# Attention and mixture-of-experts kernel: the first values come ahead of the first keys in the prologue

## The reference, cut to what matters

```python
x = x + cross_attention(layernorm(x), ctx)      # 8 heads of 64
x = x + moe_ffn(layernorm(x))                   # 8 experts, top 2, and a shared expert

# cross_attention(x, ctx):
q = x @ Wq; k = ctx @ Wk; v = ctx @ Wv          # Wq 256x512, Wk and Wv 192x512
attn = softmax(q k^T / 8); out = (attn @ v) @ Wout + bout
```

## Time and profile before

| | |
|---|---|
| median of 3 runs | 1103.0 us (1100.59 to 1103.97) |
| the profiled execution, its own time | 1101.89 us |
| its span, first to last instruction | 1100.1 us |
| PE busy | 1060.9 us, 96% of the span |
| DVE, ACT, POOL busy | 741.5, 692.6, 709.1 us |
| mean granted TensorE clock | 0.986 of full speed |

### The profile page before, as it was taken

The page is one execution under the profiler, slowest core; times in us unless marked ns, Lnnn a source line. Parts: engine busy times, 40 slices in busy tenths (PEclk is TensorE's granted clock), DMA queues, the critical chain, the costliest instruction groups (busy, mean ns, idle before and its releaser), DMA issues. The chain is left out here.

```text
span 1100.1 us, 25508 instructions
## 1 busy us (share of the span) xinstructions
PE 1060.9 (96%) x7342; PEld 928.8 (84%) x7342; DVE 741.5 (67%) x1937; ACT 692.6 (63%) x1649; POOL 709.1 (64%) x661
## 2 busy tenths in 40 slices
PE   5899999999999999999999889999999999999996
PEld 4688888888888888888887789999888888888886
DVE  3688888888888888888888767656533433433432
ACT  4788888888888888888887554332344343343442
POOL 2988898889888988898888556655033323332233
PEclk9999999999999999999999998989999999999999
DMA  7114313431343134313522285223483354334861
GB/s 216 47 32 140 124 55 99 139 124 53 101 139 120 55 103 139 120 52 105 177 90 76 98 293 187 97 76 126 136 225 57 55 136 90 55 55 64 266 175 15
DMA packets 83985, 124.06 MB, mean 113 GB/s; under 512 B 7904, under 2 KB 48080, under 8 KB 83920
## 3 DMA queue, kind: packets, MB, share of 16 engines
q1 hardware_dynamic: 63664, 99.86, 28.0%
q0 software_dynamic: 11760, 15.15, 7.7%
q10 hardware_dynamic: 8496, 8.22, 2.6%
HBM read 74.44 MB, written 49.68 MB: 113 GB/s over the span
## 5 line engine op out<-in xcount | busy, mean ns | idle before, releaser
L563 POOL TENSOR_TENSOR probs<-probs,first_rows 112x750 f32<-112x750 f32 x128 | 184.0, 1438 | 64.3 <-DVE first_rows L1020 63.2
L1802 POOL DMA_INDIRECT out<-stage,to_row x48 | 74.9, 1560 | 177.4 <-ACT stage L1854 125.9
L2083 DVE TENSOR_TENSOR hT_lo<-banks,hT_hi 128x512 fp32r<-128x512 f32 x63 | 43.6, 692 | 185.1 <-ACT hT_hi L1846 179.2
L755 ACT ACTIVATE probs<-banks,first_rows 112x375 f32<-112x375 f32 x256 | 145.2, 571 | 17.7 <-DVE first_rows L1007 15.5
L1007 DVE TENSOR_REDUCE first_rows<-banks 112x2 f32<-112x750 f32 x128 | 119.6, 935 | 28.1 <-PE banks L1392 26.3
L520 POOL TENSOR_TENSOR v_both<-v_raw,v_both 125x512 fp32r<-125x512 f32 x96 | 123.6, 1288 | 7.5
L1013 DVE TENSOR_TENSOR pT<-banks,pT 125x672 fp32r<-125x672 f32 x128 | 108.8, 850 | 17.9 <-ACT pT L746 16.7
L516 POOL TENSOR_TENSOR v_both<-v_raw,one 125x512 fp32r<-125x512 f32 x96 | 110.7, 1153 | 12.7 <-ACT v_raw L668 12.6
L1406 PEld LDWEIGHTS banks<-pT,v_both 125*128 125x128 f32 x768 | 99.6, 192 | 17.4 <-issue 9.3
L1406 PE MATMUL banks<-pT,v_both 125*128 125x224 f32 x768 | 110.7, 280 | 2.2 <-DVE oT_lo L1038 1.7
L1418 PE MATMUL banks<-ident,probs 112*125 112x112 f32 x768 | 106.7, 275 | 2.1 <-POOL probs L563 1.3
(11 more groups left out here) (287 smaller groups left out, 3067.8 us busy)
## 6 DMA issues: line engine op xcount, KB each, us to landing
w_split_scratch<-stage SPq DMA_DIRECT2D x16, 1536.0 KB, 6.6
ring<-w_split_scratch SPq DMA_DIRECT2D x16, 1536.0 KB
stage<-in_L_ffn_W SPq DMA_DIRECT2D x48, 256.0 KB, 2.9
ctx_in<-in_ctx SPq DMA_DIRECT2D x32, 376.0 KB, 3.8
xg<-x_sorted_scratch ACTq DMA_DIRECT2D x59, 136.0 KB
x_in<-in_x SPq DMA_DIRECT2D x16, 224.0 KB, 3.3
x_res<-in_x SPq DMA_DIRECT2D x32, 112.0 KB, 2.1
x_scratch<-x SPq DMA_DIRECT2D x32, 112.0 KB, 1.9
```

Source lines behind the costliest of these rows:

```text
L563: pool.tensor_tensor(probs[:, two, :], probs[:, two, :], inv_sum[:, 2 * s:2 * s + 2].rearrange("p (e o) -> p e o", o=1).to_broadcast([N, 2 ...
L755: act.activation(probs[:, h % 4, :], S_BANKS[0:N, e, 0:M], ACT.Exp, bias=neg_max[:, h:h + 1], accum_out=row_sum[:, h:h + 1]).then_inc(exp_ ...
```

## The change

The prologue's order is changed, and with it the order of the loads, of the splits of the weights and of who makes them. The two value units now come first, the first two key units second, then `xt`, then the other two key units, then `q0`. `AW` is renumbered, so that weights 0 and 1 are Wv and 2 and 3 are Wk. SP loads Wv, Wk, `x`, Wq, context 1, Wout, bias, and then the shared expert's weights, without waiting. ACT splits weights 0 to 5 before its first unit, normalises ahead of `k00`, and splits Wout after the prologue. DVE makes the low parts of all eight weights, 0 to 3 ahead of the statistics, 4 and 5 behind them, 6 and 7 at the prologue's end; POOL makes none.

```diff
-PROLOGUE = ["k00", "k10", "k20", "k30", "xt", "v00", "v10", "q0"]
+PROLOGUE = ["v00", "v10", "k00", "k10", "xt", "k20", "k30", "q0"]
-        AW = [("k", 0), ("k", 1), ("v", 0), ("v", 1), ("q", 0), ("q", 1), ("o", 0), ("o", 1)]
+        AW = [("v", 0), ("v", 1), ("k", 0), ("k", 1), ("q", 0), ("q", 1), ("o", 0), ("o", 1)]
@@ SP
             load_ctx(0, 0)
+            load_weight(Wv, 0, "v", True)
+            load_weight(Wk, 2, "k", True)
             sp.dma_start(x_in[:], x_rows(0, 2)).then_inc(x_loaded, 16)
-            load_weight(Wk, 0, "k", True)
-            load_weight(Wv, 2, "v", True)
             load_weight(Wq, 4, "q", False)
+            load_ctx(1, 1)
             (Wout, bias)
-            load_ctx(1, 1)
+            load_expert(sp, Ws1, Ws3, Ws2, weights_in[1])
             (router, x_res, wait xn_ready, x_in, wait ctx_lo_ready, contexts 2 and 3)
-            load_expert(sp, Ws1, Ws3, Ws2, weights_in[1])
@@ POOL
             rstd_of(1)
-            split_lo(pool, 2)
             for n, name in enumerate(PROLOGUE):
                 (split_values of the value units)
-            for n in (6, 7):
-                split_lo(pool, n)
@@ ACT
             ctx_hi(0, 1)
+            for i in range(6):
+                split_hi(i)
             for n, name in enumerate(PROLOGUE):
-                if name == "xt":
+                if name == "k00":
                     normed(1)
-                for i in {"k00": range(6), "k10": (6, 7)}.get(name, ()):
-                    split_hi(i)
                 (unit)
                 if name == "k30":
                     ctx_hi(1, 1)
+            for i in (6, 7):
+                split_hi(i)
@@ DVE
+            ctx_lo(0, 1)
+            for i in range(4):
+                split_lo(dve, i)
             statistics(1)
+            for i in (4, 5):
+                split_lo(dve, i)
             for n, name in enumerate(PROLOGUE):
-                if name == "k00":
-                    ctx_lo(0, 1)
-                    for i in (0, 1, 3):
-                        split_lo(dve, i)
-                    for i in (4, 5):
-                        split_lo(dve, i)
                 (unit of all but values; ctx_lo(1, 1) after k30)
+            for i in (6, 7):
+                split_lo(dve, i)
@@ PE
+                if name == "v00":
+                    pe.wait_ge(ctx_lo_ready[0], 1)
+                    pe.wait_ge(aw_lo["v"], 2)
                 if name == "k00":
-                    pe.wait_ge(ctx_lo_ready[0], 1)
                     pe.wait_ge(aw_lo["k"], 2)
-                if name == "v00":
-                    pe.wait_ge(aw_lo["v"], 2)
```

## The result

| | before | after |
|---|---|---|
| median (4 runs each) | 1103.43 us | 1094.33 us |
| range | 1100.59 to 1103.97 | 1092.91 to 1097.37 |
| ratio, 95% interval | | 0.9934, 0.9912 to 0.9956 |
| profiled execution, span | 1101.89, 1100.1 | 1097.37, 1095.3 |

The ratio is 7.3 us of 1103 (4.9 to 9.7); the two medians lie 9.1 apart. The forecast was 7.2, at 1095.8.

The account below looks back on a forecast made before the run. PE bounds the attention loop; before it, PE's waits and a POOL backlog of some 3 us delay the first turning. Moving that from 36.12 to 28.9 wins 7.2, kept to the end: 1103.0 - 7.2 = 1095.8 us, range 1092.5 to 1100.3.

Parts of the forecast that it names:

- Start, 9.0: PE's first product: Wv lands at about 6.5, 2.5 to the product, so PE starts at 9.0, 0.8 earlier.
- Value pair, 4.4: The two value units, first on PE: at most 4.6, taken as 4.4, made at 13.4.
- Key pair, 2.4: First two key units on PE, behind the value pair: 2.4, made at 15.8.
- Rows just in time: Normalised rows at `xt`: `rstd` at 13.6, at most 14.5, rows ready at 15.6; PE's wait of 2.64 goes.
- Context 1, `k21` at 21.35 after a new wait: `k21` needs context 1's low part from DVE at 21.3: PE idles 1.3, opens it at 21.35 instead of 24.25.
- First scores 23.45, `k11` 25.5, first turning 28.9, second 34.3: PE's times into the loop: scores before 27.11, `k11` 30.41, turnings of probabilities 36.12 and 41.48; 7.2 us won.
- Expert weights: Loads issued some 10 us earlier, there before 20, ACT asks at 23.85; `k11`'s wait 0.5 instead of 1.69.
- Residual rows at 19.6: `x_res` lands behind the expert's weights at 19.6; POOL wants it at 19 and has until 23.
- The clock: PE's granted clock in the new prologue: idle times of 0.6, 1.3 and 0.5, all shorter than 2.64 and 1.69.
- first rival: The clock falls in the new prologue too, 1.6 us per slow stretch; 1098.2 us, chance 0.24.
- The backlog's rival: ACT, DVE or POOL holds the first body, or a new wait appears: gain 0 to 3.7, 1101, chance 0.11.

Follow-up runs that it names:

- r3_ctx_early: Changed kernel with context 1's split moved from behind `k30` to behind `xt` on ACT and DVE; ratio to before 0.9944, run again 0.9925.
- r1_load_late: Changed kernel with the loads of the shared expert's weights put back behind SP's waits; ratio to before 1.0001.
- r4_xres_late: Changed kernel with the two loads of the residual rows `x_res` moved behind contexts 2 and 3; ratio to before 0.9932.
- n3_rows_load: Kernel before with rows normalised ahead of the first key unit, context 1 loaded ahead of Wout and expert weights right behind the bias; ratio 0.9991.
- n2_load: Kernel before with the change's load order alone: context 1 ahead of Wout, expert weights right behind the bias; ratio 1.0016.
- second group: The runs r1_load_late, r2_wout_pool, r3_ctx_early and r4_xres_late, on another chip, beside their own runs of the kernel before, median 1089.68 us.
- n5_load_filled: n2_load with 14 added products of 512 columns on PE ahead of the first turning, changing no value; ratio to before 0.9992.
- n1_rows: Kernel before with one step moved: ACT normalises the first rows ahead of its first key unit instead of ahead of `xt`; ratio 0.9973.
- n4_rows_load_lows: n3_rows_load with all low parts of the attention weights on DVE, none on POOL, keys still first; ratio to before 0.9955.
- a1_after: The changed kernel itself run once more, in the third group of runs; ratio to before 0.9940.
- r2_wout_pool: Changed kernel with Wout's two low parts given back to POOL, behind the value units; ratio to before 0.9945.

## Why the prediction was right

The total (7.2 for 7.3 in the ratio, 7.0 in the last rows) stands on steps that mostly held, the mechanism among them: PE with ACT is the later chain at the first turning, POOL just in time. That single times came so near is in part luck. PE started 0.8 earlier than forecast, the key pair took 0.4 longer, and the rest went in steps of 0.1 to 0.2 behind it; in other executions with this order of the prologue the first scores stand up to 0.7 to either side.

- *Start, 9.0.* It was 8.19: Wv was there for ACT at 5.65, not 6.5. Among the runs of the new order PE started between 8.19 and 9.24, so this term is one execution's landing. The third load of Wv was there 3.3 us behind its issue at 2.33; I had carried over the 4.4 of Wk. In this run the lead was used up again behind it.
- *Value pair, 4.4.* 12.58 - 8.19 = 4.39.
- *Key pair, 2.4.* 15.39 - 12.58 = 2.8, as the second key pair of the old kernel (2.77). The term was too small by 0.4.
- *Rows just in time.* POOL's four small instructions took 2.4, ACT waited 0.78 for them and PE 0.32; they ended at 14.53, on the bound of 14.5 that I gave and beyond the 13.6 that I took.
- *Context 1, `k21` at 21.35 after a new wait.* 21.32, waited 1.12. The trade of 2.64 for this was foreseen; r3_ctx_early shows that it could have been spared for a wait of 0.60 at `v20`.
- *First scores 23.45, `k11` 25.5, first turning 28.9, second 34.3.* 23.40, 25.72, 29.07, 34.32. The division on POOL ended at 28.65 (28.4), so PE was the later chain by 0.4.
- *Expert weights.* The step of the most weight, by r1_load_late, and in the prediction only "a wait of 0.5 instead of 1.69". In the sum it was right; as a statement of what the change lives from it was under-told.
- *Residual rows at 19.6.* They came at 20.97, and the two additions took 2.03: POOL was free at 23.0, 1.7 before it was asked again. The limit of 23 for their landing was about right, as r4_xres_late shows.
- *The clock.* The windows of the changed kernel read 1.00 up to 60 us, with idle times of 0.32, 0.35, 1.12 and 0.70:

```profile
19.00:21.30 2.30, 1.19 (x11) 1.00 (x9) 1.99 (x4) 2.30 (x6) 0.57 (x2) 1.00 0.80 186
21.30:25.00 3.70, 3.69 (x20) 2.69 (x20) 3.08 (x4) 1.85 (x4) 1.96 (x3) 1.00 0.46 129
25.00:29.00 4.00, 3.30 (x25) 2.67 (x25) 2.90 (x9) 3.69 (x10) 4.00 (x4) 1.00 0.57 189
```

So the first rival did not happen. By the rule quoted from the Trainium skill ("TensorE: Matmul & The Clock Gate", "A second HAM failure mode: psum-queue depth-cycling") it would have; the trace does not agree with that for these four idle times. The size I gave it, 1.6 us for one stretch, is what n3_rows_load lost (1.5), but a stretch can be twice as long: 2.8 in n2_load, where I had no row for that.

- *The backlog's rival.* From the second turning to the last rows the distance went from 7.16 to 7.0.

What stays open: why the second group's chip ran all kernels about 11 us faster than the others (its last rows stand where those of the other chip do, so it is in the expert stage; no trace of the kernel before was taken there); what the order of units is worth without the order of loads; and whether r3_ctx_early is faster in whole time.

## What to carry to other kernels

Ahead of a loop that one engine fills, find the first step of that loop that needs two chains, write down when each chain gets there, and price a change by the later one; an edit that moves only the earlier chain gains nothing, and an edit that is worthless alone can be worth everything once the other chain is short. Check also what the earlier chain's engine does while it waits: here one idle time of PE of 3.2 us cost another 1.5 (n3_rows_load) to 2.8 us (n2_load) behind it, so a part of a change can be slower than no change.

## What the hardware showed that I had not expected

- The granted clock fell in or up to 1.5 us behind idle times of PE of 2.64 or 2.65 (before, n2_load, n5_load_filled), 3.21 (n2_load), 3.19 (n3_rows_load), 3.61 (n1_rows), 6.54 (r1_load_late), and 1.69 (before); it did not with 1.55 (n4_rows_load_lows), 1.43 (r4_xres_late) and 1.53 (a1_after). Shorter idle times, of 0.4 to 1.1, stood ahead of all of them but the 2.64 and 2.65.
- It then stayed at its lower level for some 3.3 us (before, n1_rows, n3_rows_load), 6.6 (n2_load, from 35.8, within the wait) or 10.7 (r1_load_late, from 26.2, within the wait, to 36.9).
- PE started between 8.19 and 9.24 us in the eight profiled executions of the new order, which have the same code up to there. ACT's first split of Wv stood between 5.65 and 6.71, each time 2.5 ahead of it: the landing of the first weights alone varies by 1 us.
- Behind the loads the traces repeat closely: from the first scores to the first turning the new order took 5.66 or 5.67 us in the five traces without a wait for POOL or an edit of its work, and 5.84 in r2_wout_pool.
